# Cross-attention softmax: a separate pass of maxima per batch against an online softmax in blocks of one head group over 1024 keys

## What is computed

```python
def _L0_xattn_ref(q, k, v, wq, bq, wk, bk, wv, bv, wo, bo):      # k = v = the context, q = layernorm(x)
    qh = (q @ wq + bq).reshape(b, -1, 16, 32).transpose(0, 2, 1, 3)
    kh = (k @ wk + bk).reshape(b, -1, 16, 32).transpose(0, 2, 1, 3)
    vh = (v @ wv + bv).reshape(b, -1, 16, 32).transpose(0, 2, 1, 3)
    score = jax.nn.softmax(jnp.einsum('bhqd,bhkd->bhqk', qh, kh) / sqrt(32), axis=-1)
    out = jnp.einsum('bhqk,bhkd->bhqd', score, vh)
    return out.transpose(0, 2, 1, 3).reshape(b, -1, 512) @ wo + bo
```

## Time and profile before

| | before |
|---|---|
| time, median of 3 (lowest to highest) | 3335.28 us (3335.01 to 3337.17) |
| span of the profiled execution, first to last instruction | 3332.6 us |
| TensorE matmul, busy | 3315.3 us, 99% |
| TensorE weight loads, busy | 2661.9 us, 80% |
| VectorE / ScalarE / GpSimd, busy | 2431.5 (73%) / 1300.5 (39%) / 2110.4 (63%) us |
| granted TensorE clock, mean | 1.000 |
| DMA queue of the kernel, share of 16 engines | 18.5% |

### The profile page before, as it was taken

The page is one execution under the profiler, slowest core; times in us unless marked ns, Lnnn a source line. Parts: engine busy times, 40 slices in busy tenths (PEclk is TensorE's granted clock), DMA queues, the critical chain, the costliest instruction groups (busy, mean ns, idle before and its releaser), DMA issues.

```text
span 3332.6 us, 81287 instructions
## 1 busy us (share of the span) xinstructions
PE 3315.3 (99%) x32145; PEld 2661.9 (80%) x32145; DVE 2431.5 (73%) x3790; ACT 1300.5 (39%) x1809; POOL 2110.4 (63%) x1537
## 2 busy tenths in 40 slices
PE   9999999999999999999999999999999999999999
PEld 6777777777777777777777777778888888888888
DVE  6566676666766766677676676767887688789997
ACT  3244444444444444444444444454213322321111
POOL 3277978879788798797987979862555000033332
PEclk9999999999999999999999999999999999999999
DMA  4111111111121111111111111122122423310000
GB/s 166 60 39 49 40 52 58 37 52 39 49 58 40 52 38 51 58 40 49 46 46 56 39 52 52 43 81 77 64 99 102 137 83 108 129 66 20 25 19 19
DMA packets 211351, 199.06 MB, mean 60 GB/s; under 512 B 11520, under 2 KB 168560, under 8 KB 209520
## 3 DMA queue, kind: packets, MB, share of 16 engines
q1 hardware_dynamic: 211056, 194.50, 18.5%
HBM read 156.32 MB, written 38.13 MB: 58 GB/s over the span
## 4 chain that ended last, share of the span: by engine, by line
PE 96%; DVE 3%; issue 0%; POOL 0%; ACT 0%; DMA 0%; SPq 0%; DVEq 0%; POOLq 0%
PE a_bank L101 70%; PE a_bank L1725 7%; PE a_bank L1697 7%; PE a_bank L1688 6%; PE a_bank L790 1%; PE a_bank L1677 1%; PE a_bank L2723 1%; PE a_bank L801 0%; PE a_bank L865 0%; PE a_bank L1713 0%; PE a_bank L1744 0%; PE a_bank L839 0%; PE a_bank L2696 0%; PE a_bank L1737 0%; PE a_bank L2219 0%
## 5 line engine op out<-in xcount | busy, mean ns | idle before, releaser
L1473 DVE TENSOR_REDUCE x_maxima<-a_bank 128x1 f32<-128x512 f32 x960 | 616.3, 684 | 331.0 <-PE a_bank L1688 331.0
L1344 ACT ACTIVATE x_probsT<-x_probsT 128x1024 f32<-128x1024 f32 x480 | 509.2, 1061 | 810.1 <-DVE x_probsT L1484 810.1
L101 PE MATMUL a_bank<-x_ctx,x_wk 128*128 128x512 f32 x3072 | 770.9, 400 | 0.0
L101 PE MATMUL a_bank<-x_wv,x_ctx 128*128 128x512 f32 x3072 | 743.7, 391 | 0.0
L101 PEld LDWEIGHTS a_bank<-x_ctx,x_wk 128*128 128x128 f32 x3072 | 557.7, 188 | 157.3 <-issue 32.6
L101 PEld LDWEIGHTS a_bank<-x_wv,x_ctx 128*128 128x128 f32 x3072 | 573.2, 188 | 130.4 <-ACT x_v L1326 5.4
L1484 DVE TENSOR_TENSOR x_probsT<-a_bank,x_shift_all 128x1024 f32<-128x1024 f32 x480 | 583.4, 1216 | 2.0 <-PE a_bank L1697 1.7
L1047 POOL TENSOR_TENSOR x_pairs<-x_probsT 128x1024 f32<-128x1024 f32 x240 | 576.7, 2403 | 12.9 <-ACT x_probsT L1344 10.8
L1238 POOL TENSOR_TENSOR x_ctx<-x_tile_raw,x_one 128x512 fp32r<-128x512 f32 x236 | 245.3, 1039 | 294.3 <-PE a_bank L101 292.7
L1510 DVE SCALAR_TENSOR_TENSOR x_k<-a_bank,x_bk,x_k 128x512 fp32r<-128x512 f32 x240 | 180.2, 751 | 305.7 <-ACT x_k L1333 305.7
L1240 POOL TENSOR_TENSOR x_ctx<-x_tile_raw,x_ctx 128x512 fp32r<-128x512 f32 x236 | 301.6, 1278 | 18.5
(11 more groups left out here) (224 smaller groups left out, 4458.1 us busy)
## 6 DMA issues: line engine op xcount, KB each, us to landing
x_tile_raw<-in_ctx SPq DMA_DIRECT2D x236, 256.0 KB, 3.1
x_shift_all<-shifts SPq DMA_DIRECT2D x60, 256.0 KB, 3.6
m_ff_src<-in_w_ff SPq DMA_DIRECT2D x44, 192.0 KB, 2.5
wq_ff<-m_ff_dst SPq DMA_DIRECT2D x44, 192.0 KB, 1.8
attT<-x_out SPq DMA_DIRECT2D x32, 256.0 KB, 2.0
s_attT<-attT SPq DMA_DIRECT2D x16, 512.0 KB, 4.2
m_w_raw<-in_w SPq DMA_DIRECT2D x32, 256.0 KB, 3.0
f_w_in<-wq_ff SPq DMA_DIRECT2D x22, 256.0 KB, 3.4
```

The lines of the kernel that those rows point to most:

```text
L101: mm = pe.matmul(out, lhs[a], rhs[b], start=first and n == 0, stop=last and n == 2)
L1344: act.activation(half, half, ACT.Exp).then_inc(exped, 1)
L1473: dve.tensor_reduce(maxima[:, c, g * HG + j:g * HG + j + 1], banks[:, j], AX.X, ALU.max).then_inc(maxed, 1)
```

## The change

The attention works in 128 blocks, 8 to a batch: a block is one head group over half of the keys (1024, 8 tiles). A block's transposed scores are copied to SBUF (`keep_scores`). VectorE takes their maximum over the 8 tiles (`fold`), TensorE turns the four folded tiles (`turn_folds`), VectorE reduces them over the remaining 128 keys, negates (`shift_columns`), TensorE turns the result (`turn_shift`), and it goes through memory as before, now once a block. ScalarE copies the loaded row to PSUM (`make_table`), VectorE adds it in place (`add_shift`), and ScalarE takes exponentials over two heads at a time. The second half of a head group uses the larger of both maxima, and the sums of the first are scaled down by the exponential of the difference (`drop`, `ease`). The pass `top`, `first_top`, its maxima, the query and key halves for it, and the separate form of the last batch are gone. Key and value items run three blocks ahead, also for batch 0, of which the prologue now makes six and six. The last three blocks run without items, with parts of the next layer's first steps between them.

The core of the diff, new functions first:

```diff
+            def keep_scores(s, h):
+                act.wait_ge(scored, START + s.count(2, h + 1))
...
+                for two in (slice(0, 2), slice(2, HG)):
+                    act.activation(scores_of(s)[:, two, cols(h, TPC)],
+                                   bank[:, two].rearrange("p j (t s) -> p j t s", t=TPC), ACT.Copy).then_inc(kept, 1)
+            def make_table(e):
+                act.wait_ge(shift_loaded, START + e.count(16, 16))
...
+                act.activation(bank[:, table_bank(e)], staged[:].rearrange("p j s -> p (j s)"),
+                               ACT.Copy).then_inc(table_made, 1)
+            def fold(s, h):
+                dve.wait_ge(kept, START + s.count(HG, 3 + h))
...
+                dve.tensor_reduce(folds[:, cols(h, 2)], scores_of(s)[:, cols(h, 2)].rearrange("p j t s -> p j s t"),
+                                  AX.X, ALU.max).then_inc(folded, 1)
+            def shift_columns(s):
...
+                dve.tensor_reduce(columns(s)[:, :, new], bank[:, misc_bank(s)].rearrange("p (j s) -> p j s", j=HG),
+                                  AX.X, ALU.max).then_inc(shift_cols, 1)
...
+                dve.tensor_reduce(columns(s)[:, :, 0], columns(s)[:, :, 2:new + 1], AX.X, ALU.max,
+                                  negate=True).then_inc(shift_cols, 1)
+            def add_shift(e, j):
...
+                dve.tensor_tensor(here, here, row.to_broadcast([P, BLOCK_TILES, S]), ALU.add).then_inc(shifted, 1)
```

VectorE's step, GpSimd's and TensorE's:

```diff
+                if e2.exists():
+                    gather(s, e2)
+                if e3.exists():
+                    gather_den(s, e3)
+                if e1.exists():
+                    add_shift(e1, 0)
+                    add_shift(e1, 1)
+                if s.exists():
+                    fold(s, 0)
+                    fold(s, 1)
+                if e1.exists():
+                    add_shift(e1, 2)
+                if s.exists():
+                    shift_columns(s)
+                if e1.exists():
+                    add_shift(e1, 3)
...
+                if e2.exists():
+                    add_up(e2)
+                if e1.exists() and e1.half:
+                    ease(e1)
+                if e4.exists() and e4.half:
+                    normalise(e4)
+                if s.at == 4 and past.exists():
+                    finish(past)
+                if s.ahead(TILES_AHEAD).exists():
+                    split_tiles(s)
...
+            def turn_folds(s):
+                pe.wait_ge(folded, START + s.count(2, 2))
...
+                for j in range(HG):
+                    mm = pe.transpose(bank[:, misc_bank(s), cols(j, S)], folds[:, j], id_t[:])
+                mm.then_inc(folds_turned, 1)
+            def items(s):
+                m = s.ahead(ITEMS_AHEAD)
...
+                key_item(m, 0, KEY_BANK)
...
+                value_item(m, 0, VALUE_BANK)
...
+                key_item(m, 1, KEY_BANK, (2, lambda: turn_folds(s)))
...
+                value_item(m, 1, VALUE_BANK, (0, lambda: turn_shift(s)))
+            def strips(s):
+                e2, e3 = s.back(2), s.back(3)
+                if s.exists():
+                    score(s, 0)
+                if e2.exists():
+                    weigh(s, e2)
+                if e3.exists():
+                    sum_up(s, e3)
+                if s.exists():
+                    score(s, 1)
```

More of the change, by code:

```diff
@@ L318, with __init__, ahead, back @@
 UNROLL = 4
+PER_BATCH = 8
+RING = 3
+PERIOD = PER_BATCH * RING
+BLOCKS = B * PER_BATCH
+class Block:
+    def __init__(self, n, k):
+        self.n, self.k = n, k
+        self.group, self.half, self.at = k % HG, k % PER_BATCH // HG, k % PER_BATCH
+        self.turn = k // PER_BATCH
+    def ahead(self, d):
+        return Block(self.n + (self.k + d) // PERIOD, (self.k + d) % PERIOD)
+    def back(self, d):
+        return self.ahead(-d)
+    def count(self, per=1, plus=0):
+        return self.n * (PERIOD * per) + (self.k * per + plus)
+    def batch(self):
+        return self.n * RING + self.turn if isinstance(self.n, int) else None
+    def batches(self, per=1, plus=0):
+        return self.n * (RING * per) + (self.turn * per + plus)
+    def seconds(self, per=1, plus=0):
+        return self.n * (PERIOD // 2 * per) + ((self.turn * HG + self.group) * per + plus)
+    def ring(self):
+        return self.k % RING
+    def number(self):
+        return self.n * PERIOD + self.k if isinstance(self.n, int) else None
+    def exists(self):
+        return not isinstance(self.n, int) or 0 <= self.number() < BLOCKS
+    def from_end(self):
+        return self.number() - BLOCKS if isinstance(self.n, int) else -BLOCKS
+def run_blocks(nc, eng, step, until):
+    for k in range(PERIOD):
+        step(Block(0, k))
+    with looped(nc, eng, 1, BLOCKS // PERIOD) as n:
+        for k in range(PERIOD):
+            step(Block(n, k))
+    for k in range(BLOCKS // PERIOD * PERIOD, until):
+        step(Block(k // PERIOD, k % PERIOD))
 class Tile:
@@ L1458, in _ @@
+            for c in range(2):
+                late.weights_hi(act, 4, c)
             late.scalar(act)
@@ L1639, in _, with end_step @@
-            late.weights_lo(dve, 4, 1)
-            late.turned_lo(dve, FIRST)
-            late.vector(dve, invert_last, normalise_last)
+            for m in range(1, B // MT):
+                q.normalise(dve, m)
+                q.turned_lo(dve, m)
+            run_blocks(nc, dve, step, BLOCKS - ITEMS_AHEAD)
+            def end_step(k):
+                step(Block(k // PERIOD, k % PERIOD))
+            end_step(BLOCKS - 3)
+            end_step(BLOCKS - 2)
+            late.add_input(dve, FIRST)
@@ L1642, in _ @@
+            late.vector(dve)
             late.after.vector(dve)
@@ L1859, in _ @@
[L1859 to L1872 removed]
+            pe.wait_ge(ctx_made, START + 2)
@@ new lines, in _, with end_step, end_turns @@
+            for g in range(2):
+                pe.wait_ge(v_ready, START + g + 3)
+                key_item(Block(0, 2), g, 6 + g)
+            q.project(pe, 2)
+            q.turn(pe, 3)
+            for v in range(2):
+                pe.wait_ge(k_ready, START + v + 5)
+                value_item(Block(0, 2), v, 6 + v)
+            q.project(pe, 3)
+            run_blocks(nc, pe, step, BLOCKS - ITEMS_AHEAD)
+            def end_step(k):
+                step(Block(k // PERIOD, k % PERIOD))
+            def end_turns(k):
+                s = Block(k // PERIOD, k % PERIOD)
+                turn_folds(s)
+                turn_shift(s)
```

1215 lines of the change are left out of this document (473 added, 742 removed).

## The result

The changed kernel takes 3756.1 us (median of 4 runs, 3745.6 to 3759.5), the kernel before 3336.1 us (3335.0 to 3337.2) on the same chip: a ratio of 1.125, with a 95% interval of 1.1237 to 1.1269. It is slower by 420 us, on the side and by the mechanism that was forecast, and 107 us beyond the point of 3649 us, 3 us inside the upper end of the range.

The account below looks back on a forecast made before the run. TensorE bounded the kernel before; in the changed one its wait for VectorE's slow folds would set the step. 96 + 125 x 19.36 + 85 + 1045 = 3646 us of span, with 2.7 us 3649 us; range 3238 to 3759.

Parts of the forecast that it names:

- the floor: Loop step on TensorE's work alone, with 0.1 us of semaphore waits: 16.2 us.
- The fold's term: VectorE's reduce of 2048 gapped elements for two heads, at 1.85 ns each plus 143 ns fixed: 3.93 us.
- The slope of 1.54 ns: Price per gapped element on VectorE, from small reduces of 4 to 32 elements; it gave a fold of 3.30 us.
- The contiguous end: VectorE's fold with no price on gaps, at 1.04 ns an element: 2.28 us.
- 7 ns a result: Counter-reading of VectorE's small reduces: price per result, not per gap, costing nothing in folds with 8 elements a result.
- 11.5 + 2F: Loop step in us when TensorE waits for VectorE's two folds of F each: 19.4 us with F = 3.93.
- The walk: Following one loop step from its first score strip through TensorE and VectorE; TensorE stands 3.1 us at `turn_folds`.
- The tail: Last three blocks, without items to cover their chains, to the end of the split weights and products: 85 us.
- Gaps for nothing: Rival: gaps cost VectorE's folds nothing, 2.28 us each, TensorE bounds again, 3245 us, faster; chance 0.18.
- The fold between: Rival: VectorE's fold takes about 2.7 us, steps 16.9 us, about 3334 us, same; chance 0.03.
- The memory trip: Rival: with fast folds, the shift's way through memory closes the loop, 17.0 us steps, about 3346 us; chance 0.03.
- GpSimd as bound: Rival: GpSimd's adds cost a third more and set steps of 17.5 us, 3407 us; chance 0.02.

Follow-up runs that it names:

- the filled kernel: The changed kernel with 18 more transposes of the identity, read by nobody, in front of each `turn_folds`; 3636.2 us, 1.0907 of the kernel before.
- e12_between: The changed kernel with folds through PSUM, a new GpSimd order in the tail, `turn_folds` and `turn_shift` a quarter item later; 3283.2 us, 0.9841 of the kernel before.

## Why the prediction was right, and where its number was short

**The side and the mechanism were right.** VectorE, off the path before, sets the step through the fold; nothing hides it, as the next fold waits for scores behind it. The test is the removal of the gap alone, which takes 469 us away and leaves steps at the floor.

**The fold's term.** 3.93 us forecast, 3.83 measured: 1.80 ns an element, between the two prices of 1.78 and 1.92 from reduces of 32 and 64 elements. The slope of 1.54 ns that made the lower bound was off. The contiguous end (2.28) was measured at 2.279. What spoke against the term, 7 ns a result in place of a price on gaps, is refuted by the run without a gap.

**The step, 11.5 + 2F.** With the measured fold it gives 19.16 us; the steps at full clock last 18.81. With the short fold it gives 16.2 by the floor; measured 16.20. With 5.3 us of fold in place of 2F it gives 16.8 and measured is 16.4: 0.35 and 0.4 us too long. The walk charged a little too much between the strips and the folds.

**What was missing in the step is the clock.** The prediction counted TensorE's wait as its only cost. In 104 of the 125 steps the clock was also halved for 3.4 us from about the end of the wait, and the steps went from 18.81 to 19.95 on average. That is 1.14 x 125 = 143 us, the largest error of the sum. In the loop of the kernel before TensorE had no wait and the clock no such stretch; the filled kernel shows that the stall is its cause. So the steps are 0.8 us off 11.5 + 2F, which the prediction named as a sign of being wrong, by two errors that partly cancel.

**The tail, 85 us forecast and 118.1 measured.** A tail of over 100 us was named beforehand as a sign that the prediction is wrong, and in this term it is. The walk followed each block's own chain and left out the orders of the queues at the end. VectorE's `add_input` waited 12.70 us behind GpSimd's `add_up(125)` for a bias add of 1.26 us, so the turn of block 127 waited 16.28 us. `add_up(126)` waited on GpSimd behind the layer norm of the first tile, and two `sum_up`s waited 8.60 and 7.88 us. With the contiguous fold the tail is 111.2 us where 76 were forecast, short by as much (35 and 33 us), so the length of the fold doesn't explain it. Two changes of order gave 16 us back; the other half was not taken apart: the chain of block 127 has no cover in any version, and TensorE's clock over the tail is 0.69 in the changed kernel.

**The sum.** Prologue +2.1 (98.1 for 96), fold 125 x -0.20 = -25, the rest of the step's walk 125 x -0.35 = -44, clock +143, tail +33.1, rest +2.8: 112 us, from 3646 to 3757.7 us of span. That the time lies in the range, 3 us inside its end, is luck: the end was made for folds of 4.36 us, and the folds took 3.83. What reached up to it were the clock and the tail, which the sum did not have, and they would have gone past it by some 66 us if the fold and the walk had not been overestimated by 69.

**The rivals.** Gaps for nothing: refuted as a fact and confirmed as a price (3245 forecast, 3286.8 measured without gaps, of which 35 is the tail and 7 the prologue). The fold between: the kernel through PSUM is such a case, 2.65 us for two heads, and 3315.9 us. The memory trip: with fast folds and the old place TensorE has no wait on it; with the transposes half an item later VectorE's adds wait for the table 0.20 us a step (17.7 us over 90 steps), beside the larger wait in VectorE's own order. GpSimd as bound: it stands 704 us waiting for exponentials in the changed kernel, and in `e12_between`, with steps of 16.27 us, it ended no wait of TensorE in the 125 steps.

## What to carry to other kernels

Before work is moved to an engine with room, price it in the access pattern that it will have there: a one-operand reduce with its reduced axis outermost costs 1.8 instead of 1.04 ns an element, and the same maxima made from contiguous pieces, one operand in PSUM, turned 12.5% slower into 0.6% faster (the tail's order and a later place of the transposes gave the last percent). A stall of TensorE in every step may cost more than its length: look at the granted clock behind it. Here a stall of 2.23 us cost 1.14 us more by the clock, and one split into 1.33 and 0.57 us nothing more. Where an epilogue is written out by hand, walk each engine's queue in order, not each block's chain.

## What the runs showed of the hardware that was not expected

- A gap of 16 bytes costs the reduce as much as one of 512 (3834 and 3832 ns for 2048 elements; 256 folds in one execution of each).
- VectorE's elementwise maximum of two SBUF operands took 0.69 us for 512 results with GpSimd standing and 0.74 to 2.78 with it running; with one operand in PSUM it took 680 to 697 ns, running or not.
- Strides of 32 bytes between elements took VectorE's add from 1213 to 2294 ns, ScalarE's copy from 1023 to 2234, TensorE's product with 128 moving columns from 276 to 413, GpSimd's sum with one such operand from 2396 to 3172, but its sum with two from 2373 down to 2059. For kernels of one's own on GpSimd the Trainium skill ("GPSIMD Engine Reference", section 7) has half as much again per element for reads with steps over 8 bytes; the trace of these built-in adds shows a third more in the one case and 13% less in the other.
- More instructions made the kernel faster: 2250 transposes that nobody reads gave 120 us, by the clock.
- The same wait of TensorE, 2.2 us, was followed by half clock in 104 steps and not in 21.
